# C products of a selective scan in pairs of states, with the sixteen states of a unit dealt anew to VectorE, GpSimd and TensorE

## The chip, the cores and the metric

One core of one Trainium2 chip runs the whole program in one launch. The metric is the time on the device in microseconds, the median of the runs. Engines: TensorE (PE in the profile, PEld its weight loads), VectorE (DVE), ScalarE (ACT), GpSimd (POOL) and SyncE (SP), which issues the transfers.

## The reference, cut to what matters

A layer norm, a scan over channels and a bidirectional selective scan (Mamba) with 2048 inner channels, 16 states, 4096 tokens, then gating and an output projection. The part that the change touches is this, once forward and once backward over the tokens:

```python
def step(h, inp):
    u_t, dt_t, B_t, C_t = inp
    dA = jnp.exp(dt_t[:, :, None] * A)
    h = dA * h + (dt_t * u_t)[:, :, None] * B_t[:, None, :]
    y = jnp.einsum('bdn,bn->bd', h, C_t)
    return (h, y)
```

All data are 32-bit floats.

## The kernel before

The scan stage (`stage_scan`) works in 256 units: 128 of the backward direction, then 128 of the forward one. A unit is one block of 128 channels by one chunk of 512 tokens; 16 units make a chunk. For each state n of 16, ScalarE writes `da` = exp(A·delta) to one of two PSUM slots (L1074), GpSimd has made `w` = du·B for four states in one instruction (L1179), and VectorE runs the scan over the 512 tokens (L1231). Then h times C has to be summed over the states into `yT`, a PSUM tile in which TensorE adds transposes.

Three groups of states do this in three ways:

- VN, ten states: the scan writes `h` in PSUM (two slots), VectorE multiplies by C into one of six `hc` slots (`weigh`, L1241), TensorE adds the transpose (L962).
- PN, four states: the scan writes `hs` in SBUF (four slots shared with TN), GpSimd multiplies by C into `hp` (`weigh_c`, L1188), TensorE adds the transpose (L923).
- TN, two states: the scan writes `hs`, TensorE turns it into `in_ps` (`turn`, L858), ScalarE copies that to `h_turned` (`turn_copy`, L1040), and TensorE multiplies it by a diagonal of C into `yT` (`add_turned`, L867).

Every engine has its own program, in order, with the place of each piece of work given by the state number n at which it stands. On ScalarE, step n of unit b is `save(b, n)` (L1054), which keeps the last column of state n-2 for the next chunk and waits for that scan; then the exponential of state n; then whatever stands at n: at 0 the copy `proj_copy` once a chunk; at 1 the diagonals of the convolution and `dt_read`; at 2 `yT_copy` of the unit before; at 2, 4, 5 and 6 the chain that gives `delta` of the next unit; at 7 `in_copy` (L1014); at 10 `ud` (L1106) and `xc_copy` (L1017); at 12 and 15 the two `turn_copy`. So no exponential is started before all that stands ahead of it, and it is at most two states ahead of the scans.

On TensorE, step n of a unit has: at 0 and 2 the two halves of the input projection (`in_step`, L836), at 5 the convolution (L843), at 8 and 12 the two turns, at 11 the projection `proj` (L848) and `ud` (L954), at 12 and 15 `add_turned` (the one at 12 ahead of the turn at 12), at 13 the `dt` product of a later unit (L831; at 0 in the last unit of a chunk), at the POOL_AT steps the sum of `hp`, and at the end of each step of a VN state the sum of its `hc`, for which the whole queue waits. `in_ps` and `dt_ps` are one PSUM bank each.

GpSimd's unit is: `w` of group 2, C product, `w` of group 3, C product, `u` and `du` of the next unit (L1163, L1166), C product, `w` 0 of the next unit, C product, `w` 1 of the next unit; in the first unit of a chunk two diagonals of C (L1154) besides.

A product of VectorE waits for its scan, for a free `hc` slot, and for the `save` of its state (`h_saved`): the wait names the count of step n+2 of ScalarE, which is the step that saves n.

SyncE issues all loads and stores in program order; it holds for `du_done`, `yT_copied`, `in_copied`, `xc_copied` and `proj_mm` of each unit in that order.

In the last 16 of the backward units (112 to 127) no input projection is left to do; the forward units 128 to 238 have again an input projection (of z) and a convolution for later units.

Of the kernel before, what the change touches and what calls it, by code (L numbers as in the profile page):

```python
# [9 lines left out]
P = 128  # L10
# [7 lines left out]
NS = 16  # L18
# [10 lines left out]
PN = [2, 5, 8, 11]  # L29
TN = [4, 10]  # L30
# [3 lines left out]
NHS = 4  # L34
# [514 lines left out]
def stage_scan(nc, ident, hnT_d, winx_d, winz_d, wx_d, wdt_d, convp_d, par_d, skip_d,  # L549
               x_pad_d, xc_d, z_d, bc_d, yT_d):  # L550
    with Scope(nc, "scan") as sc:
# [18 lines left out]
        delta, u, du = (sc.sb(n, [P, 2, T]) for n in ("delta", "u", "du"))  # L570
# [4 lines left out]
        hs, hp = sc.sb("hs", [P, NHS, T]), sc.sb("hp", [P, NP, T])  # L575
# [43 lines left out]
        def h_slot(b, n):  # L619
            if n in SN:  # L620
                return hs[:, (b * NSN + SN.index(n)) % NHS]
            return h[:, (b * NV + VN.index(n)) % 2]
# [31 lines left out]
        POOL_AT = [5, 8, 11, 14]  # L654
# [171 lines left out]
        def _(pe):  # L826
# [89 lines left out]
            def unit(b):  # L916
                ins = inputs_of(b)
                for n in range(NS):
                    if n in POOL_AT:
                        i = POOL_AT.index(n)  # L920
# [58 lines left out]
        def _(act):  # L979
# [88 lines left out]
            def unit(b):  # L1068
                s, nxt, ins = b % 2, b + 1 < NU, inputs_of(b)
                for n in range(NS):  # L1070
# [11 lines left out]
                    if n == 2:  # L1082
                        yT_copy(b - 1)
# [18 lines left out]
                    if n == 10:  # L1102
                        act.wait_ge(S["skip_loaded"], 2 * DB * LOAD)
                        act.wait_ge(S["u_done"], b + 1)
                        act.wait_ge(S["yT_copied"], b + 1)
                        nc.scalar.activation(ud[:], u[:, s], ACT.Copy,  # L1106
                                             scale=skip[:, block_of(b):block_of(b) + 1]).then_inc(S["ud_done"], 1)
# [39 lines left out]
        def _(pool):  # L1147
# [10 lines left out]
            def scan_input(b):  # L1158

                s = b % 2  # L1160
                pool.wait_ge(p_in[s], (b // 2 + 1) * (NPL * LOAD))
                hold(pool, S["ud_done"], b + 1, S["passed"])
                nc.gpsimd.tensor_scalar(u[:, s], xc[:, s], 10.0, -10.0, ALU.min, ALU.max).then_inc(S["u_done"], 1)  # L1163
                pool.wait_ge(S["u_done"], b + 1)
                pool.wait_ge(S["delta_done"], b + 1)
                nc.gpsimd.tensor_tensor(du[:, s], delta[:, s], u[:, s], ALU.mult).then_inc(S["du_done"], 1)  # L1166

            def weigh_b(b, g, single=False):

                s = b % 2  # L1170
# [3 lines left out]
                if single:  # L1174
                    for i in range(G):
                        nc.gpsimd.tensor_tensor(w[:, g, i], du[:, s], bcast_b[:, g * G + i],
                                                ALU.mult).then_inc(S["w_done"], 1)
                else:
                    nc.gpsimd.tensor_tensor(w[:, g], du[:, s].unsqueeze(1).to_broadcast([P, G, T]),  # L1179
                                            bcast_b[:, g * G:(g + 1) * G], ALU.mult).then_inc(S["w_done"], G)  # L1180

            def weigh_c(b, i):

                n = PN[i]
                pool.wait_ge(c_loaded[n // G], (b // DB + 1) * LOAD)
                pool.wait_ge(S["scan_done"], b * NS + (n + 1 + SCR))
                pool.wait_ge(S["hp_used"], b * NP + i + 1)
                nc.gpsimd.tensor_tensor(hp[:, i], h_slot(b, n), bcast_c[:, n], ALU.mult).then_inc(S["hp_done"], 1)  # L1188

            def unit(b):  # L1190
# [4 lines left out]
                weigh_c(b, 1)  # L1195
                if nxt:
                    scan_input(b + 1)
                weigh_c(b, 2)
# [3 lines left out]
                if nxt:  # L1202
                    weigh_b(b + 1, 0)
                weigh_c(b, 3)
                if nxt:
                    weigh_b(b + 1, 1)

# [10 lines left out]
        def _(dve):  # L1218
            def scan(b, n):
# [14 lines left out]
            def weigh(b, n):  # L1234
                i = VN.index(n)
                dve.wait_ge(c_loaded[n // G], (b // DB + 1) * LOAD)
                dve.wait_ge(S["scan_done"], b * NS + n + 1 + SCR)
                dve.wait_ge(S["hc_used"], b * NV + i + 1)
# [267 lines left out]
```

## Time and profile before

| | |
|---|---|
| median of 3 runs | 8327.16 us (8322.33 to 8331.08) |
| profiled execution, its own time | 8327.64 us |
| its span, first to last instruction | 8325.9 us |
| busy share: TensorE, VectorE, ScalarE, GpSimd | 87%, 87%, 64%, 81% |
| first scan of the stage starts at | 775.6 us |
| last scan starts at | 7279.1 us |
| mean granted TensorE clock | 0.948 |

Busy shares are of the whole span; the scan stage is 78% of it and its own shares are higher. An instruction's duration in the profile is longer than the time until the next one starts, since instructions of one engine overlap by up to 0.1 us; where several follow one another without a wait, the difference of their starts is what one costs. The clock is told as a share of 2.4 GHz; it has two levels, 2.4 and 1.2 GHz, and the figure is the mean over a stretch.

### The profile page before, as it was taken

Reading aid. Unit: us, or ns where it says so; the run is one execution under the profiler, and the core shown is the slowest. Engines: PE = TensorE matmul, PEld = TensorE weight load, DVE = VectorE, ACT = ScalarE, POOL = GpSimd, SP = SyncE. Lnnn points to the kernel's source line nnn. Section 1 sums busy time; section 2 is a strip of 40 time slices with the busy share of each in tenths; the row PEclk is TensorE's granted clock in tenths of the full one; section 3 lists DMA queues with packets and bytes.
Section 4 is the critical chain, followed back from the end, with each engine's and each line's share of the span. In section 5 each row is a group of like instructions: output and inputs, shape, how many; then the busy total and the mean of one; then the engine's idle time right before and its main releaser. Section 6 shows DMA issues by size and latency. Waiting matters only on the chain. (4 is left out here: it accounts for less than half of the span.)

```text
span 8325.9 us, 116063 instructions
## 1 busy us (share of the span) xinstructions
PE 7232.1 (87%) x32656; PEld 4473.8 (54%) x32656; DVE 7202.0 (87%) x7790; ACT 5330.5 (64%) x12487; POOL 6737.9 (81%) x2833
## 2 busy tenths in 40 slices
PE   7568989998999899977899899899888987779999
PEld 3243555555555555555555555555555555534444
DVE  6921999999999999999999999999999999934444
ACT  3743777777777777776777777777777776610000
POOL 0612999999999999999999999999999999921110
PEclk9789999999999999988899999999999998889999
DMA  3273232313232323221323232323232322154342
GB/s 86 76 199 135 66 117 69 117 66 117 69 117 66 117 69 117 67 98 43 105 76 127 80 129 75 128 80 127 76 128 81 124 98 82 44 199 139 134 141 75
DMA packets 540822, 843.96 MB, mean 101 GB/s; under 512 B 112576, under 2 KB 260032, under 8 KB 522816
## 3 DMA queue, kind: packets, MB, share of 16 engines
q1 hardware_dynamic: 540224, 837.03, 30.5%
q8 instruction: 248, 4.06, 0.2%
q14 instruction: 350, 2.87, 0.1%
HBM read 583.83 MB, written 253.02 MB: 101 GB/s over the span
## 5 line engine op out<-in xcount | busy, mean ns | idle before, releaser
L1179 POOL TENSOR_TENSOR scan_w<-scan_du,scan_bcast_b 128x2048 f32<-128x2048 f32 x1023 | 4633.4, 4541 | 3.6 <-DMA scan_bcast_b<-bc 3.6
L1231 DVE TENSOR_TENSOR_SCAN scan_h<-scan_da,scan_state,scan_w 128x512 f32<-128x512 f32 x2560 | 3178.7, 1280 | 36.6 <-ACT scan_da L1074 21.3
L1074 ACT ACTIVATE scan_da<-scan_delta,scan_prm 128x512 f32<-128x512 f32 x4096 | 2804.3, 685 | 0.0
L962 PE MATMUL scan_yT<-all_ident,scan_hc 128*128 128x128 f32 x10240 | 1514.7, 279 | 768.1 <-DVE scan_hc L1241 767.5
L962 PEld LDWEIGHTS scan_yT<-all_ident,scan_hc 128*128 128x128 f32 x10240 | 1184.8, 142 | 1447.9 <-DVE scan_hc L1241 1068.5
L1231 DVE TENSOR_TENSOR_SCAN scan_hs<-scan_da,scan_state,scan_w 128x512 f32<-128x512 f32 x1536 | 1906.1, 1265 | 59.4 <-PE scan_in_ps L858 41.0
L836 PE MATMUL scan_in_ps<-scan_hn,scan_win 128*128 128x512 f32 x3840 | 1730.8, 593 | 13.5 <-issue 13.5
L1241 DVE TENSOR_TENSOR scan_hc<-scan_h,scan_bcast_c 128x512 f32<-128x512 f32 x2560 | 1652.5, 678 | 38.4 <-ACT scan_state L1054 36.7
L1188 POOL TENSOR_TENSOR scan_hp<-scan_hs,scan_bcast_c 128x512 f32<-128x512 f32 x1024 | 1306.5, 1276 | 60.0 <-issue 54.1
L836 PEld LDWEIGHTS scan_in_ps<-scan_hn,scan_win 128*128 128x128 f32 x3840 | 693.1, 191 | 714.7 <-issue 714.7
L1054 ACT ACTIVATE scan_state<-scan_h 128x1 f32<-128x1 f32 x2560 | 433.4, 169 | 868.6 <-DVE scan_h L1231 861.3
L843 PE MATMUL scan_dt_ps<-scan_x,scan_diag 128*128 128x512 f32 x1920 | 899.4, 612 | 1.1 <-ACT scan_x L1014 1.1
L1390 PE MATMUL out_o_ps<-out_yg,out_wout 128*128 128x512 f32 x2048 | 892.6, 595 | 0.0
L1358 POOL TENSOR_TENSOR out_yf<-out_yf,out_yb 128x512 f32<-128x512 f32 x128 | 162.9, 1273 | 740.5 <-DMA out_z<-z 740.5
L923 PE MATMUL scan_yT<-all_ident,scan_hp 128*128 128x128 f32 x4096 | 644.2, 282 | 2.8 <-POOL scan_hp L1188 2.5
L1390 PEld LDWEIGHTS out_o_ps<-out_yg,out_wout 128*128 128x128 f32 x2048 | 386.5, 191 | 465.8 <-issue 465.8
L1368 ACT ACTIVATE out_sz<-out_z 128x512 f32<-128x512 f32 x128 | 80.7, 630 | 822.2 <-DMA out_z<-z 822.2
L867 PE MATMUL scan_yT<-scan_h_turned,scan_c_diag 128*128 128x128 f32 x4096 | 594.4, 293 | 0.0
L843 PEld LDWEIGHTS scan_dt_ps<-scan_x,scan_diag 128*128 128x128 f32 x1920 | 355.9, 196 | 383.9 <-issue 383.9
L867 PEld LDWEIGHTS scan_yT<-scan_h_turned,scan_c_diag 128*128 128x128 f32 x4096 | 560.4, 212 | 0.0
L1040 ACT ACTIVATE scan_h_turned<-scan_in_ps 128x512 f32<-128x512 f32 x512 | 300.6, 587 | 338.4 <-PE scan_in_ps L858 338.4
L923 PEld LDWEIGHTS scan_yT<-all_ident,scan_hp 128*128 128x128 f32 x4096 | 499.2, 146 | 8.2 <-POOL scan_hp L1188 6.8
(128 smaller groups left out, 6761.9 us busy)
## 6 DMA issues: line engine op xcount, KB each, us to landing
yT<-scan_y_out SPq DMA_DIRECT2D x257, 256.0 KB, 2.0
scan_win<-winx SPq DMA_DIRECT2D x128, 512.0 KB, 3.6
xc<-scan_xc_out SPq DMA_DIRECT2D x256, 256.0 KB, 2.0
scan_xc<-xc SPq DMA_DIRECT2D x256, 256.0 KB, 3.9
scan_bcast_b<-bc SPq DMA_DIRECT2D x64, 1024.0 KB, 8.3
scan_bcast_c<-bc SPq DMA_DIRECT2D x64, 1024.0 KB, 7.7
scan_win<-winz SPq DMA_DIRECT2D x128, 512.0 KB, 4.7
scan_x<-x_pad SPq DMA_DIRECT2D x128, 257.5 KB, 2.6
```

The source lines that it names most:

```text
L836: last = nc.tensor.matmul(bank, win[:, s, i], hn[:, i], start=(i == 0), stop=(i == KT - 1))
L843: last = nc.tensor.matmul(bank, diag[:, s, i], x[:, s, at:at + T], start=(i == 0), stop=(i == TAPS - 1))
L867: last = nc.tensor.matmul(yT[:, tb], c_diag[:, k, tb], h_turned[:, tb * P:(tb + 1) * P], start=False, stop=False)
L923: last = nc.tensor.matmul(yT[:, tb], hp[:, i, tb * P:(tb + 1) * P], ident[:], is_transpose=True, start=False, stop=False)
L962: last = nc.tensor.matmul(yT[:, tb], hc_slot(b, n)[:, tb * P:(tb + 1) * P], ident[:], is_transpose=True, start=(i == 0 and tb == 0), stop= ...
L1054: nc.scalar.activation(state_of(unit_, n_), h_slot(unit_, n_)[:, col:col + 1], ACT.Copy).then_inc(S["h_saved"], 1)
L1074: nc.scalar.activation(da[:, n % 2], delta[:, s], ACT.Exp, scale=decay(b, n)).then_inc(S["exp_done"], 1)
L1179: nc.gpsimd.tensor_tensor(w[:, g], du[:, s].unsqueeze(1).to_broadcast([P, G, T]), bcast_b[:, g * G:(g + 1) * G], ALU.mult).then_inc(S["w_d ...
L1188: nc.gpsimd.tensor_tensor(hp[:, i], h_slot(b, n), bcast_c[:, n], ALU.mult).then_inc(S["hp_done"], 1)
L1231: nc.vector.tensor_tensor_scan(flip(b, h_slot(b, n)), flip(b, da[:, n % 2]), flip(b, w[:, n // G, n % G]), state_of(b, n), ALU.mult, ALU.a ...
L1241: nc.vector.tensor_tensor(hc_slot(b, n), h_slot(b, n), bcast_c[:, n], ALU.mult).then_inc(S["hc_done"], 1)
L1390: last = nc.tensor.matmul(o_ps[:, q % 2], wout[:, q, b], yg[:, g, b], start=(b == 0), stop=(b == DB - 1))
```

## The change

- The states are dealt anew: PN = 0, 1, 10, 13; TN = 4, 7; VN = 2, 3, 5, 6, 8, 9, 11, 12, 14, 15, five pairs of neighbours. `hs` has one slot for each of its six states instead of four in turn; `delta` keeps two slots, `u` and `du` have one.
- VectorE multiplies two states by C in one instruction of 128x1024, right after scans 4, 7, 10 and 13, which write SBUF; the pair 14, 15 is multiplied after scan 0 of the next unit. The wait for `h_saved` becomes that for the second state of the pair, n+1.
- GpSimd multiplies 0 and 1 in one instruction and 10 and 13 in another; its order is `w` 2, pair, `w` 3, `u`, `du`, `w` 0, `w` 1, pair.
- TensorE takes `hp` at steps 5, 8, 14, 14 instead of 5, 8, 11, 14.
- ScalarE: `yT_copy` moves from step 2 to 4 and `ud` from 10 to 5. `turn_steps` (the turns at 8 and 12, their copies at 12 and 15) and every other step stay as they are.

```diff
-PN = [2, 5, 8, 11]
-TN = [4, 10]
+PN = [0, 1, 10, 13]
+TN = [4, 7]
...
-NHS = 4
+HS = {0: 0, 1: 1, 4: 2, 7: 3, 10: 4, 13: 5}
...
-        delta, u, du = (sc.sb(n, [P, 2, T]) for n in ("delta", "u", "du"))
+        delta, u, du = sc.sb("delta", [P, 2, T]), sc.sb("u", [P, T]), sc.sb("du", [P, T])
...
-        hs, hp = sc.sb("hs", [P, NHS, T]), sc.sb("hp", [P, NP, T])
+        hs, hp = sc.sb("hs", [P, NSN, T]), sc.sb("hp", [P, NP, T])
...
-                return hs[:, (b * NSN + SN.index(n)) % NHS]
-            return h[:, (b * NV + VN.index(n)) % 2]
+                return hs[:, HS[n]]
+            return h[:, VN.index(n) % 2]
...
-        POOL_AT = [5, 8, 11, 14]
+        POOL_AT = [5, 8, 14, 14]
...
-                    if n == 2:
+                    if n == 4:
                         yT_copy(b - 1)
...
-                    if n == 10:
+                    if n == 5:
                         act.wait_ge(S["skip_loaded"], 2 * DB * LOAD)
...
-                hold(pool, S["ud_done"], b + 1, S["passed"])
-                nc.gpsimd.tensor_scalar(u[:, s], xc[:, s], 10.0, -10.0, ALU.min, ALU.max).then_inc(S["u_done"], 1)
+                hold(pool, S["ud_done"], b + 2, S["passed"])
+                nc.gpsimd.tensor_scalar(u[:], xc[:, s], 10.0, -10.0, ALU.min, ALU.max).then_inc(S["u_done"], 1)
...
             def weigh_c(b, i):
-                n = PN[i]
-                pool.wait_ge(c_loaded[n // G], (b // DB + 1) * LOAD)
-                pool.wait_ge(S["scan_done"], b * NS + (n + 1 + SCR))
-                pool.wait_ge(S["hp_used"], b * NP + i + 1)
-                nc.gpsimd.tensor_tensor(hp[:, i], h_slot(b, n), bcast_c[:, n], ALU.mult).then_inc(S["hp_done"], 1)
+                first, second = PN[i], PN[i + 1]
+                for n in (first, second):
+                    pool.wait_ge(c_loaded[n // G], (b // DB + 1) * LOAD)
+                pool.wait_ge(S["scan_done"], b * NS + (second + 1 + SCR))
+                pool.wait_ge(S["hp_used"], b * NP + i + 2)
+                nc.gpsimd.tensor_tensor(hp[:, i:i + 2], hs[:, HS[first]:HS[first] + 2],
+                                        bcast_c[:, first:second + 1:second - first], ALU.mult
+                                        ).then_inc(S["hp_done"], 2)
             def unit(b):
                 nxt = b + 1 < NU
                 weigh_b(b, 2)
                 weigh_c(b, 0)
                 weigh_b(b, 3)
-                weigh_c(b, 1)
-                if nxt:
-                    scan_input(b + 1)
-                weigh_c(b, 2)
                 if b % DB == 0:
                     for k in range(NTN):
                         make_diagonal(b, k)
                 if nxt:
+                    scan_input(b + 1)
                     weigh_b(b + 1, 0)
-                weigh_c(b, 3)
-                if nxt:
                     weigh_b(b + 1, 1)
+                weigh_c(b, 2)
...
-                if n in SN:
-                    g = b * NSN + SN.index(n) - NHS
-                    if g >= 0 and SN[g % NSN] in PN:
-                        dve.wait_ge(S["hp_done"], g // NSN * NP + PN.index(SN[g % NSN]) + 1 + NP)
-                    elif g >= 0:
-                        dve.wait_ge(S["h_turn_mm"], g // NSN * NTN + TN.index(SN[g % NSN]) + 1)
-                else:
+                if n in PN:
+                    dve.wait_ge(S["hp_done"], b * NP + PN.index(n) + 1)
+                elif n in TN and b:
+                    dve.wait_ge(S["h_turn_mm"], (b - 1) * NTN + TN.index(n) + 1)
+                elif n in VN:
                     dve.wait_ge(S["hc_done"], b * NV + VN.index(n) + 1)
...
+            def weigh(b, i):
+
+                n, at = VN[i], (b * NV + i) % NOUT
+                for m in (n, n + 1):
+                    dve.wait_ge(c_loaded[m // G], (b // DB + 1) * LOAD)
+                dve.wait_ge(S["scan_done"], b * NS + n + 2 + SCR)
+                dve.wait_ge(S["hc_used"], b * NV + i + 2)
                 if b + 1 < NU or n < NS - 2:
-                    dve.wait_ge(S["h_saved"], b * NS + n + 3)
+                    dve.wait_ge(S["h_saved"], b * NS + n + 4)
+                nc.vector.tensor_tensor(hc[:, at:at + 2], h[:], bcast_c[:, n:n + 2], ALU.mult).then_inc(S["hc_done"], 2)
             def unit(b):
                 for n in range(NS):
                     scan(b, n)
-                    if n in PN:
-                        ready = (n - 2, n - 1)
-                    else:
-                        ready = (n - 1, n) if n in (NS - 3, NS - 1) else ()
-                    for m in ready:
-                        if m in VN:
-                            weigh(b, m)
+                    if n == 0 and b:
+                        weigh(b - 1, NV - 2)
+                    if n in (4, 7, 10, 13):
+                        weigh(b, (n - 4) // 3 * 2)
```

## Rows read from the trace of the kernel before

**Rows 1.** Busy time by window: units 16 to 111, 112 to 127, 128 on

```profile
1180.00:3620.00 2440.00, 2200.14 (x10804) 1412.51 (x10803) 2413.43 (x2516) 1870.64 (x4553) 2414.72 (x982) 0.97 0.28 95
3624.00:4061.00 437.00, 315.64 (x1543) 220.58 (x1541) 401.75 (x418) 299.54 (x740) 400.43 (x163) 0.81 0.19 63
4061.00:7256.00 3195.00, 2828.84 (x14070) 1849.32 (x14069) 3165.66 (x3303) 2425.26 (x5895) 3166.21 (x1287) 0.96 0.29 98
```

**Rows 2.** The same windows, scans of L1231 alone (x is their count)

```profile
1180.00:3620.00 2440.00, 1887.90 (x1548) 0.97 0.28 95
3624.00:4061.00 437.00, 312.55 (x257) 0.81 0.19 63
4061.00:7256.00 3195.00, 2477.56 (x2033) 0.96 0.29 98
```

**Rows 3.** Groups by line and form: 512-wide and 1024-wide products, whole span

```profile
L1241 DVE TENSOR_TENSOR scan_hc<-scan_h,scan_bcast_c 128x512 f32<-128x512 f32 x2560 | 1652.5, 678 | 38.4 <-ACT scan_state L1054 36.7 <-issue 0.3
...
L347 DVE TENSOR_TENSOR norm_xn<-n_scanned,n_xt 128x1024 f32 (+1 forms) x32 | 37.2, 1203 | 0.0
...
L302 POOL TENSOR_TENSOR norm_xn<-norm_xn,norm_rstd 128x1024 f32 x28 | 65.4, 2355 | 0.0
```

**Rows 4.** Longest wait of VectorE in the scan stage: us in total, times, longest

```profile
DVE scan_hs L1231 <- PE scan_in_ps L858: 41.0, 66, 1.9
```

**Rows 5.** Timeline of VectorE, end of unit 50

```profile
2078.87 2.46 DVE L1231 TENSOR_TENSOR_SCAN scan_h<-scan_da,scan_state,scan_w 128x512 f32<-128x512 f32 x2
2081.23 1.27 DVE L1241 TENSOR_TENSOR scan_hc<-scan_h,scan_bcast_c 128x512 f32<-128x512 f32 x2
2082.42 2.46 DVE L1231 TENSOR_TENSOR_SCAN scan_h<-scan_da,scan_state,scan_w 128x512 f32<-128x512 f32 x2
...
2085.97 1.28 DVE L1231 TENSOR_TENSOR_SCAN scan_h<-scan_da,scan_state,scan_w 128x512 f32<-128x512 f32 x1
```

**Rows 6.** Timeline of GpSimd, unit 50

```profile
2067.73 4.53 POOL L1179 TENSOR_TENSOR scan_w<-scan_du,scan_bcast_b 128x2048 f32<-128x2048 f32 x1
2072.22 1.26 POOL L1188 TENSOR_TENSOR scan_hp<-scan_hs,scan_bcast_c 128x512 f32<-128x512 f32 x1
...
2075.49 1.28 POOL L1188 TENSOR_TENSOR scan_hp<-scan_hs,scan_bcast_c 128x512 f32<-128x512 f32 x1
```

**Rows 7.** Timeline of TensorE, unit 50

```profile
2062.81 3.60 PE L836 MATMUL scan_in_ps<-scan_hn,scan_win 128*128 128x512 f32 x8
2066.25 1.04 PE L962 MATMUL scan_yT<-all_ident,scan_hc 128*128 128x128 f32 x8
...
2071.56 3.67 PE L843 MATMUL scan_dt_ps<-scan_x,scan_diag 128*128 128x512 f32 x8
...
2079.01 0.66 PE L962 MATMUL scan_yT<-all_ident,scan_hc 128*128 128x128 f32 x4 [2.03 <-DVE scan_hc L1241]
2079.50 0.60 PE L923 MATMUL scan_yT<-all_ident,scan_hp 128*128 128x128 f32 x4
...
2081.23 1.06 PE L867 MATMUL scan_yT<-scan_h_turned,scan_c_diag 128*128 128x128 f32 x8
2082.12 0.60 PE L858 MATMUL scan_in_ps<-all_ident,scan_hs 128*128 128x128 f32 x4
...
2083.09 1.12 PE L831 MATMUL scan_dt_ps<-scan_proj,scan_wdt 64*128 64x512 f32 x2
```

**Rows 8.** Timeline of ScalarE, unit 50: copies, saves and exponentials

```profile
2070.82 0.60 ACT L1014 ACTIVATE scan_x<-scan_in_ps 128x512 f32<-128x512 f32 x1 [0.60 <-PE scan_in_ps L836]
2071.31 0.17 ACT L1054 ACTIVATE scan_state<-scan_h 128x1 f32<-128x1 f32 x1
2071.36 0.70 ACT L1074 ACTIVATE scan_da<-scan_delta,scan_prm 128x512 f32<-128x512 f32 x1
...
2082.76 0.60 ACT L1040 ACTIVATE scan_h_turned<-scan_in_ps 128x512 f32<-128x512 f32 x1 [0.65 <-PE scan_in_ps L858]
```

**Rows 9.** Timeline of TensorE in unit 122, where the clock is lower

```profile
3907.50 5.30 PE L843 MATMUL scan_dt_ps<-scan_x,scan_diag 128*128 128x512 f32 x8
```

More of the change, by code:

```diff
@@ L918, in unit @@
                 for n in range(NS):
-                    if n in POOL_AT:
-                        i = POOL_AT.index(n)
+                    for i in range(NP):
+                        if n != POOL_AT[i]:
+                            continue
                         pe.wait_ge(S["hp_done"], b * NP + i + 1 + NP)
@@ L1105, in unit @@
                         act.wait_ge(S["yT_copied"], b + 1)
-                        nc.scalar.activation(ud[:], u[:, s], ACT.Copy,
+                        nc.scalar.activation(ud[:], u[:], ACT.Copy,
                                              scale=skip[:, block_of(b):block_of(b) + 1]).then_inc(S["ud_done"], 1)
@@ L1161, in scan_input @@
                 pool.wait_ge(p_in[s], (b // 2 + 1) * (NPL * LOAD))
-                hold(pool, S["ud_done"], b + 1, S["passed"])
-                nc.gpsimd.tensor_scalar(u[:, s], xc[:, s], 10.0, -10.0, ALU.min, ALU.max).then_inc(S["u_done"], 1)
+                hold(pool, S["ud_done"], b + 2, S["passed"])
+                nc.gpsimd.tensor_scalar(u[:], xc[:, s], 10.0, -10.0, ALU.min, ALU.max).then_inc(S["u_done"], 1)
                 pool.wait_ge(S["u_done"], b + 1)
                 pool.wait_ge(S["delta_done"], b + 1)
-                nc.gpsimd.tensor_tensor(du[:, s], delta[:, s], u[:, s], ALU.mult).then_inc(S["du_done"], 1)
+                nc.gpsimd.tensor_tensor(du[:], delta[:, s], u[:], ALU.mult).then_inc(S["du_done"], 1)
             def weigh_b(b, g, single=False):
-                s = b % 2
                 pool.wait_ge(S["du_done"], b + 1)
@@ L1175, in weigh_b @@
                     for i in range(G):
-                        nc.gpsimd.tensor_tensor(w[:, g, i], du[:, s], bcast_b[:, g * G + i],
+                        nc.gpsimd.tensor_tensor(w[:, g, i], du[:], bcast_b[:, g * G + i],
                                                 ALU.mult).then_inc(S["w_done"], 1)
                 else:
-                    nc.gpsimd.tensor_tensor(w[:, g], du[:, s].unsqueeze(1).to_broadcast([P, G, T]),
+                    nc.gpsimd.tensor_tensor(w[:, g], du[:].unsqueeze(1).to_broadcast([P, G, T]),
                                             bcast_b[:, g * G:(g + 1) * G], ALU.mult).then_inc(S["w_done"], G)
             def weigh_c(b, i):
-                n = PN[i]
-                pool.wait_ge(c_loaded[n // G], (b // DB + 1) * LOAD)
-                pool.wait_ge(S["scan_done"], b * NS + (n + 1 + SCR))
-                pool.wait_ge(S["hp_used"], b * NP + i + 1)
-                nc.gpsimd.tensor_tensor(hp[:, i], h_slot(b, n), bcast_c[:, n], ALU.mult).then_inc(S["hp_done"], 1)
+                first, second = PN[i], PN[i + 1]
[6 more added lines that the diff above has]
+                                        ).then_inc(S["hp_done"], 2)
             def unit(b):
@@ L1232, in scan @@
                                              state_of(b, n), ALU.mult, ALU.add).then_inc(S["scan_done"], 1)
[L1234 to L1238, printed above, removed]
+            def weigh(b, i):
[4 more added lines that the diff above has]
+                dve.wait_ge(S["hc_used"], b * NV + i + 2)
                 if b + 1 < NU or n < NS - 2:
-                    dve.wait_ge(S["h_saved"], b * NS + n + 3)
-                nc.vector.tensor_tensor(hc_slot(b, n), h_slot(b, n), bcast_c[:, n], ALU.mult).then_inc(S["hc_done"], 1)
+                    dve.wait_ge(S["h_saved"], b * NS + n + 4)
+                nc.vector.tensor_tensor(hc[:, at:at + 2], h[:], bcast_c[:, n:n + 2], ALU.mult).then_inc(S["hc_done"], 2)
             def unit(b):
@@ L1266, in _ @@
                 unit(b)
+            weigh(NU - 1, NV - 2)
 def stage_out(nc, passed, ident, yf_d, yb_d, z_d, wout_d, x1T_d, out_d):
```

## The prediction

> **What bounds the kernel now.** I read the page first. Over the span no engine stands out: TensorE and VectorE are busy alike and GpSimd is close (the table of busy shares). The windows of the scan stage alone say more. In the ordinary stretches VectorE is busy 2413 of 2440 us and 3166 of 3195, and GpSimd is busy 2415 and 3166 [rows 1]. Two engines are full together, TensorE has 10% to spare, ScalarE a quarter. With the counts of scans (1548 and 2033, 16 to a unit) a unit takes 5635 / 223.8 = 25.18 us there, and 437 / 16.06 = 27.2 in the stretch without an input projection, where TensorE's granted clock is 0.81 [rows 2]. The waits of VectorE are few: 41 us for the turn that frees an `hs` slot (1.9 us a time, in the stretch with the lower clock above all) and 37 us ahead of the products for a `save` of ScalarE [rows 3, 4].
>
> The work of a unit is summed from starts, so that overlaps count. VectorE: two scans cost 2081.23 - 2078.87 = 2.36, two products 1.19 [rows 5]. So 16 x 1.18 + 10 x 0.595 = 24.8 us. GpSimd: a `w` of four states costs 4.49, a C product 1.23 (its 1.27 less the 0.04 of overlap that `w` shows), and one product with `u` and `du` 3.27 [rows 6]. So 4 x 4.49 + 3.27 + 3 x 1.23 = 24.92, and with the two diagonals once in 16 units 25.07. GpSimd is the nearer bound of 25.18; VectorE is 0.4 under it.
>
> **The products themselves.** On VectorE a product of 1024 lasts 1.203 us, one of 512 0.678 [rows 3]. The pair costs 0.595 + 0.525 = 1.12 instead of 1.19; five save 0.35 and a unit of VectorE falls to 18.88 + 5.6 = 24.45. On GpSimd 1024 elements last 2.355 [rows 3], 2.31 after overlap; two pairs save 4 x 1.23 - 2 x 2.31 = 0.30, so 24.62, with the diagonals 24.77.
>
> Here the page "VectorE: DVE Perf Modes" of the Trainium skill (section on the TRN2 errata) bears on the case: a fixed latency is paid once per instruction, and an fp32 tensor_tensor takes (N+151) cycles at 0.96 GHz. By that each instruction saved would give 0.157 us and five 0.79; by the rows a pair gives 0.07, since neighbours overlap. I use the rows.
>
> **The other edits that cost or give little.** Six `hs` slots remove the wait of 41 us. GpSimd's new order has room: the pair 10, 13 waits for scan 13 and holds back `w` 2 of the next unit, which is wanted only by scan 8; the pair 0, 1 waits for scan 1 and holds `w` 3, wanted by scan 12. From scan 13's end GpSimd needs 2.3 + 4.5 and then waits for scan 1 with nothing lost at periods over 24.8. Single `u` and `du` hold `scan_input` for `ud`, now five steps earlier: free. On SyncE `load_p` waits for `du` as before; the stores of y come 2 us later, behind `yT_copied`, with `store_x` and `store_xc` queued behind; a unit has 25 us for them, so nothing. `yT_copy` at step 4 waits for the sums of 14, 15, which are ready about a microsecond before (below): without the move it would stall.
>
> **Where the new order costs: the end of a unit.** I count from the end of the product of 11 and 12, which follows scan 13. TensorE's queue stands at step 11, at the sum of `hc` 11. Only behind it come, at step 12, `add_turned` of state 4 and then the turn of state 7. ScalarE's copy of that turn stands at step 15, ahead of the exponential of state 0 of the next unit, and scan 0 needs that. So: the sum starts 0.05 later and costs 0.49 (2079.50 - 2079.01), `add_turned` 0.89 (2082.12 - 2081.23), the turn ends 0.60 after its start [rows 7]; the copy starts 0.04 later (2082.76 after 2082.72), 0.49 to the `save`, 0.05 to the exponential, 0.70 for it [rows 8], 0.04 until the scan. Sum 3.35. VectorE itself has in this time only scans 14 and 15, 2.36 less 0.09 (the product's end lies that far behind the next start): 2.27. **Stall 1.07 us a unit.** Before, the turn came after the sum of state 9, and the products of 14 and 15 stood between scan 15 and the next unit: the same copy started at 2082.76, 3.2 us ahead of scan 0 at 2085.97 [rows 5, 8], where 1.3 is needed. The cover was those products and the earlier turn, and both are gone.
>
> **The middle of a unit.** Count from scan 0. The product of 14 and 15 starts at 1.18 and ends at 2.38. TensorE's sums of 14 and 15 with `add_turned` between: 2.43 + 0.49 + 0.89 + 0.44 = 4.25. Only then comes the next input projection, 2 x 3.44 (2066.25 - 2062.81), its end at 11.28. Before, both products were over when scan 0 began, so the projection started some 2.4 earlier. VectorE meanwhile: scan 1 at 2.30, scans 2, 3, 4, product, scans 5, 6, 7, product of 5 and 6 due at 11.68. That product needs the `save` of 6, at step 8 of ScalarE, behind `in_copy` at step 7: 11.28 + 0.04 + 0.49 + 0.17 [rows 8] + 0.04 = 12.02. **Stall 0.34.** Then TensorE sums 2 and 3 (0.87) and `hp` (0.44) and runs the convolution (3.67): from 11.13 to 16.11. `xc_copy` stands at step 10, the `save` of 9 behind it: 16.11 + 0.04 + 0.6 + 0.17 + 0.04 = 16.96; the product of 8 and 9 is due at 12.02 + 1.12 + 3.54 = 16.68. **Stall 0.28.** Where the clock is full no other exponential is late: two steps of ScalarE with one extra activation each take 1.3 a step, and a scan with its share of a product 1.5.
>
> **Sum.** 24.45 + 1.07 + 0.34 + 0.28 = 26.14 us. Once in 16 units the `dt` product (1.05, 2083.09 in [rows 7] and its 1.12) goes ahead of the input projection and shifts both middle stalls: 0.07 on the mean, 26.21. Against 25.18 that is +1.03 x 240 ordinary units = +247 us. The 16 units of the lower clock have no input projection, so the middle stalls are absent; their turn wait goes; the end chain costs 1.07, or 0.87 more if TensorE's 1.98 of it run at 5.30 / 3.67 [rows 7, 9]. About 25.9 for 27.2: -21.
>
> One term the rows of a full clock leave out: TensorE's clock. It is busy 5029 of 5635 us now, 22.5 a unit, 0.89, with a clock of 0.965; in the other stretch 0.72 with 0.81 [rows 1]. At 26.2 a unit the share is 0.86; on the line between the two the clock is 0.93, so some 6% more of the time is at 1.2 GHz. A unit wholly there would take 10.5 x 0.44 for projection and convolution and 0.87 for the end chain, 5.5 us more: 0.34 a unit, 82 us. Part of it falls where TensorE waits anyway; the bounds are 0 and 82, I take 40. All told 8328 + 247 - 21 + 40 = 8594, say 8590 (the profiled execution's own time of 8327.6 is the median within half a microsecond). Own range: each stall is known to about 0.15 (60 us together), the clock term 0 to 82: 8520 to 8680.
>
> **Rivals.**
> (A) Faster. The waits do not bind and the sums of the two full engines decide: VectorE 24.45, GpSimd 24.77. Then 240 x 0.41 + 16 x 2.4 = 137 us less, 8190. It needs the exponential of state 0 at most 2.27 us after the product of 11 and 12, that is a turn of state 7 that TensorE runs before the sum of 11. The queue in the code does not allow it; for it speaks that GpSimd, the fullest engine, is relieved. 0.09, with all that I may misread.
> (B) The end chain alone binds, the projection and convolution are in time (they lack 0.3 each): 24.45 + 1.07 = 25.52, +0.34 x 240 - 21 = +61, 8390. 0.14.
> (C) The clock falls more than on the line. The new idle time of TensorE is in two pieces, some 2.4 us ahead of the sum of 11 and 1.4 ahead of that of 14, against one of 2.03 [rows 7]; the first lies just ahead of the end chain. At a clock of 0.90, 13% more of the time at 1.2 GHz: 0.72 x 240 = +172 on 8554, 8725; at 0.81, 8960. 0.12.
> The page "TensorE: Matmul & The Clock Gate" of the Trainium skill (Part 1) says that the slow state is the default and that activity releases it; the 0.81 beside TensorE's lower busy share agrees [rows 1].
>
> **How the numbers follow.** Forecast 0.65, A 0.09, B 0.14, C 0.12. The range from 8385 to 8730 leaves out A and the slow half of C. A measurement of this kernel can tell 0.2% (17 us) from no change; no case lies there, but the lower side of B reaches it if the end chain is half as long: I give 0.04 of B's chance to the same and 0.01 to faster. Faster 0.10, same 0.04, slower 0.86.
>
> **What the profile after will show.** Products x1280 of 1.2 us on VectorE and x512 of 2.36 on GpSimd. VectorE's waits: scans of state 0 (an `hs` scan now) for ScalarE's `da`, about 1 us a unit and 250 in total; products waiting for ScalarE's `save`, twice 0.3 a unit. No wait for the turn. ScalarE's wait for the turn (L1040) and TensorE's for `hc` grow. VectorE and GpSimd both fall to some 94% of the stage. A scan 0 that starts 2.4 us after the product of 11 and 12 ends would make the prediction wrong; so would an input projection that starts before 3 us.

## The result, and the profile after

8899.75 us median of 4 runs (8897.35 to 8902.79) against 8325.49, the median of now 4 runs of the kernel before: 1.0689 times the time before, 95% interval 1.0671 to 1.0708. I had forecast 8590, with a range of 8385 to 8730. The sign and the two places in an ordinary unit were right; the 264 us that I had added were less than half of the 574 that came.

The windows of the profile after, over units 16 to 111, 112 to 127 and 128 to 239 for all engines, and then those and the units from 240 on with the scans of L1228 alone (the x of VectorE, 16 to a unit):

```profile
1240.00:3876.00 2636.00, 2211.50 (x10727) 1443.62 (x10726) 2402.58 (x2015) 1818.66 (x4510) 2374.09 (x780) 0.96 0.25 84
3877.00:4313.00 436.00, 290.21 (x1536) 209.98 (x1535) 398.96 (x336) 296.34 (x736) 395.16 (x130) 0.90 0.19 64
4314.00:7397.00 3083.00, 2586.39 (x12534) 1687.80 (x12534) 2805.26 (x2352) 2123.81 (x5265) 2772.92 (x911) 0.96 0.28 94
```

```profile
1240.00:3876.00 2636.00, 1864.83 (x1535) 0.96 0.25 84
3877.00:4313.00 436.00, 310.99 (x256) 0.90 0.19 64
4314.00:7397.00 3083.00, 2177.66 (x1792) 0.96 0.28 94
7397.00:7850.00 453.00, 310.41 (x256) 0.86 0.15 51
```

VectorE and GpSimd, full before [rows 1], are busy 91% and 90%. A unit takes 2636 / 95.9 = 27.5 us and 3083 / 112 = 27.5 where it took 25.2 [rows 2], 436 / 16 = 27.3 in the middle stretch where it took 27.2, and 453 / 16 = 28.3 in the last one. The mean granted clock of the ordinary stretches is as before, 0.96.

The groups by line, and the waits of VectorE in the scan stage:

```profile
L1240 DVE TENSOR_TENSOR scan_hc<-scan_h,scan_bcast_c 128x1024 f32<-128x1024 f32 x1280 | 1539.1, 1202 | 105.2 <-PE scan_yT L963 57.8 <-ACT scan_state L1055 46.4 <-DVE scan_h L1228 0.2
...
L1189 POOL TENSOR_TENSOR scan_hp<-scan_hs,scan_bcast_c 128x1024 f32<-128x1024 f32 x512 | 1206.5, 2356 | 585.5 <-DVE scan_hs L1228 583.9 <-issue 0.2
```

```profile
DVE scan_hs L1228 <- ACT scan_da L1075: 420.5, 257, 3.3
DVE scan_hc L1240 <- PE scan_yT L963: 57.8, 215, 1.3
DVE scan_hc L1240 <- ACT scan_state L1055: 46.4, 28, 2.7
```

The products last what the 1024-wide rows of other stages said, 1.202 and 2.356 [rows 3]. The wait for the turn [rows 4] is gone. In its place scans into `hs` wait 257 times for the exponential, once a unit, 420 us in all: that is scan 0. Of the waits ahead of products, 57.8 us are laid to the sum of an `hc` slot and 46.4 to a save; below I show that the save is the true one for both.

VectorE through unit 50 (start, duration, instruction), to set beside [rows 5]:

```profile
2175.12 1.28 DVE L1228 TENSOR_TENSOR_SCAN scan_hs<-scan_da,scan_state,scan_w 128x512 f32<-128x512 f32 x1 [2.20 <-ACT scan_da L1075]
2176.32 1.20 DVE L1240 TENSOR_TENSOR scan_hc<-scan_h,scan_bcast_c 128x1024 f32<-128x1024 f32 x1
2177.43 1.27 DVE L1228 TENSOR_TENSOR_SCAN scan_hs<-scan_da,scan_state,scan_w 128x512 f32<-128x512 f32 x1
...
2182.15 1.20 DVE L1240 TENSOR_TENSOR scan_hc<-scan_h,scan_bcast_c 128x1024 f32<-128x1024 f32 x1
2183.45 2.46 DVE L1228 TENSOR_TENSOR_SCAN scan_h<-scan_da,scan_state,scan_w 128x512 f32<-128x512 f32 x2
...
2187.31 1.22 DVE L1240 TENSOR_TENSOR scan_hc<-scan_h,scan_bcast_c 128x1024 f32<-128x1024 f32 x1 [0.23 <-PE scan_yT L963]
...
2192.22 1.20 DVE L1240 TENSOR_TENSOR scan_hc<-scan_h,scan_bcast_c 128x1024 f32<-128x1024 f32 x1
...
2197.07 1.20 DVE L1240 TENSOR_TENSOR scan_hc<-scan_h,scan_bcast_c 128x1024 f32<-128x1024 f32 x1
2198.37 2.47 DVE L1228 TENSOR_TENSOR_SCAN scan_h<-scan_da,scan_state,scan_w 128x512 f32<-128x512 f32 x2
2201.62 1.28 DVE L1228 TENSOR_TENSOR_SCAN scan_hs<-scan_da,scan_state,scan_w 128x512 f32<-128x512 f32 x1 [0.78 <-ACT scan_da L1075]
```

This unit takes 26.50 us (2201.62 - 2175.12). The next takes 28.02, and so on in turn: by the starts of the first scans, 209 ordinary units have a mean of 27.28 (25.10 before), and of them 101 take more than 27.5. Two things are to be seen here. The product that starts at 2176.32 is followed 1.11 us later by a scan into `hs`; the one at 2182.15 is followed 1.30 later by a scan into `h`, and so are those at 2192.22 and 2197.07 (after the one at 2187.31, which itself waited, it is 1.36). And from the end of the product of 11 and 12 (2197.07 + 1.20) to scan 0 it is 3.35 us.

TensorE and ScalarE at the end of unit 50 (first four rows) and of unit 51 (the rest):

```profile
2198.32 0.66 PE L963 MATMUL scan_yT<-all_ident,scan_hc 128*128 128x128 f32 x4 [2.47 <-DVE scan_hc L1240]
2198.82 1.06 PE L867 MATMUL scan_yT<-scan_h_turned,scan_c_diag 128*128 128x128 f32 x8
2199.71 0.60 PE L858 MATMUL scan_in_ps<-all_ident,scan_hs 128*128 128x128 f32 x4
...
2200.35 0.60 ACT L1041 ACTIVATE scan_h_turned<-scan_in_ps 128x512 f32<-128x512 f32 x1 [2.38 <-PE scan_in_ps L858]
...
2224.83 1.11 PE L963 MATMUL scan_yT<-all_ident,scan_hc 128*128 128x128 f32 x4 [2.46 <-DVE scan_hc L1240]
2225.74 1.91 PE L867 MATMUL scan_yT<-scan_h_turned,scan_c_diag 128*128 128x128 f32 x8
2227.44 0.88 PE L858 MATMUL scan_in_ps<-all_ident,scan_hs 128*128 128x128 f32 x4
...
2228.36 0.60 ACT L1041 ACTIVATE scan_h_turned<-scan_in_ps 128x512 f32<-128x512 f32 x1 [3.89 <-PE scan_in_ps L858]
```

The chain is the same, but in unit 51 TensorE's part lasts 3.49 us instead of 1.99. Four microseconds of each by windows (the figure behind the last engine is the granted clock):

```profile
2224.00:2228.00 4.00, 3.17 (x15) 3.17 (x16) 3.24 (x3) 0.48 (x1) 4.00 (x2) 0.57 0.47 166
2198.00:2202.00 4.00, 3.67 (x24) 2.75 (x25) 3.11 (x4) 1.65 (x5) 4.00 (x2) 1.00 0.33 92
```

In unit 51 the clock is 0.57 over the chain, that is 1.2 GHz for nearly all of it, right after 2.46 us without work. Ahead of the chain of unit 50 there is the same idle time, and it ran at 2.4 GHz. The trace's granted clock says the same of all units: the 101 long ones of the 209 each have a stretch at 1.2 GHz (28.08 us on the mean), the 108 others have none (26.53 us). In the kernel before 74 of the 209 have such a stretch too, but they take only 25.38 us against 24.95 for the rest.

### The profile page after: what moved, and what is told of

It is laid out like the page before. It is cut to its first block and busy times, and to the rows that moved or that the text cites. A ratio compares the mean times of both kernels' runs of the same rounds, so it can differ in the third digit from the quotient of the medians.

```text
span 8895.6 us, 112992 instructions
## 1 busy us (share of the span) xinstructions
PE 7317.9 (82%) x32656; PEld 4578.2 (51%) x32656; DVE 7226.4 (81%) x6510; ACT 5249.4 (59%) x12487; POOL 6688.5 (75%) x2321
## 3 DMA queue, kind: packets, MB, share of 16 engines
q1 hardware_dynamic: 540224, 837.03, 28.3%
## 5 line engine op out<-in xcount | busy, mean ns | idle before, releaser
L1228 DVE TENSOR_TENSOR_SCAN scan_h<-scan_da,scan_state,scan_w 128x512 f32<-128x512 f32 x2560 | 3150.5, 1276 | 135.5 <-ACT scan_da L1075 16.0
L963 PE MATMUL scan_yT<-all_ident,scan_hc 128*128 128x128 f32 x10240 | 1543.9, 288 | 1257.5 <-DVE scan_hc L1240 1257.5
L1228 DVE TENSOR_TENSOR_SCAN scan_hs<-scan_da,scan_state,scan_w 128x512 f32<-128x512 f32 x1536 | 1941.7, 1264 | 439.8 <-ACT scan_da L1075 420.5
L963 PEld LDWEIGHTS scan_yT<-all_ident,scan_hc 128*128 128x128 f32 x10240 | 1215.8, 147 | 1703.1 <-DVE scan_hc L1240 1453.4
L836 PE MATMUL scan_in_ps<-scan_hn,scan_win 128*128 128x512 f32 x3840 | 1692.3, 593 | 14.4 <-issue 13.5
L1189 POOL TENSOR_TENSOR scan_hp<-scan_hs,scan_bcast_c 128x1024 f32<-128x1024 f32 x512 | 1206.5, 2356 | 585.5 <-DVE scan_hs L1228 583.9
L1240 DVE TENSOR_TENSOR scan_hc<-scan_h,scan_bcast_c 128x1024 f32<-128x1024 f32 x1280 | 1539.1, 1202 | 105.2 <-PE scan_yT L963 57.8
L867 PE MATMUL scan_yT<-scan_h_turned,scan_c_diag 128*128 128x128 f32 x4096 | 674.1, 319 | 0.0
L867 PEld LDWEIGHTS scan_yT<-scan_h_turned,scan_c_diag 128*128 128x128 f32 x4096 | 629.9, 234 | 0.0
L924 PE MATMUL scan_yT<-all_ident,scan_hp 128*128 128x128 f32 x4096 | 595.1, 279 | 0.2
L924 PEld LDWEIGHTS scan_yT<-all_ident,scan_hp 128*128 128x128 f32 x4096 | 467.6, 143 | 185.2 <-issue 175.6
```

What stands on the lines that cost most here:

```text
L836: last = nc.tensor.matmul(bank, win[:, s, i], hn[:, i], start=(i == 0), stop=(i == KT - 1))
L867: last = nc.tensor.matmul(yT[:, tb], c_diag[:, k, tb], h_turned[:, tb * P:(tb + 1) * P], start=False, stop=False)
L963: last = nc.tensor.matmul(yT[:, tb], hc_slot(b, n)[:, tb * P:(tb + 1) * P], ident[:], is_transpose=True, start=(i == 0 and tb == 0), stop= ...
L1189: nc.gpsimd.tensor_tensor(hp[:, i:i + 2], hs[:, HS[first]:HS[first] + 2], bcast_c[:, first:second + 1:second - first], ALU.mult).then_inc( ...
L1228: nc.vector.tensor_tensor_scan(flip(b, h_slot(b, n)), flip(b, da[:, n % 2]), flip(b, w[:, n // G, n % G]), state_of(b, n), ALU.mult, ALU.a ...
L1240: nc.vector.tensor_tensor(hc[:, at:at + 2], h[:], bcast_c[:, n:n + 2], ALU.mult).then_inc(S["hc_done"], 2)
```

## Experiments

Two theories. **The end chain**: the sum of `hc` 11, `add_turned`, turn, ScalarE's copy and the exponential of state 0, with a clock term on top. **The rival**: the loss is in the middle of the unit and in the pairs themselves. Each run is a time and a ratio to runs of the kernel before made beside it.

### e1: the turn of state 7 one step earlier

```diff
-            return dict(mm=(8, 12), copy=(12, NS - 1), add=(12, NS - 1))
+            return dict(mm=(8, 11), copy=(12, NS - 1), add=(12, NS - 1))
```

> Theory (the end chain): the turn of state 7 stands behind the sum of hc 11 on TensorE, and scan 0 of the next unit waits for its copy. With the turn one step earlier, ahead of that sum, the 420 us that hs scans wait for the exponential go to under 30 and a unit takes 25.6 to 25.9 us: 8400 (8350 to 8480). Rival (the loss is the product's write that the next scan into the same PSUM slot waits for, 0.19 us four times a unit, and the middle of the unit): the wait moves to another place and the time stays above 8700.

Measured 8810.8 us, 1.0581 (1.0550 to 1.0612): far outside my range, and above 8700 as the rival had it. The wait of scan 0 went from 420 to 252 us, not to 30. TensorE and ScalarE at the end of unit 133:

```profile
4435.17 1.53 PE L867 MATMUL scan_yT<-scan_h_turned,scan_c_diag 128*128 128x128 f32 x8
...
4436.80 0.60 ACT L1041 ACTIVATE scan_h_turned<-scan_in_ps 128x512 f32<-128x512 f32 x1 [2.47 <-PE scan_yT L867]
```

The copy now waits for L867, `add_turned` of state 4. There is one `h_turned`, and `turn_copy` waits until it is used (`h_turned_used`); that product still stood behind the sum of `hc` 11. The chain has two links, and I had seen one. The clock hides part of what the first gives: it was 0.917 over this run against 0.945 for the changed kernel, 195 of the 209 ordinary units have a stretch at 1.2 GHz, and the 14 without one take 26.23 us, where the changed kernel takes 26.53.

### e7: both links moved

```diff
-            return dict(mm=(8, 12), copy=(12, NS - 1), add=(12, NS - 1))
+            return dict(mm=(8, 11), copy=(12, NS - 1), add=(11, NS - 1))
```

> On TensorE both the product of state 4 (add_turned) and the turn of state 7 stand at step 11, ahead of the sum of hc 11; the change has both at 12. The run with the turn alone at 11 left ScalarE's copy waiting for add_turned, which frees h_turned. Theory (the end chain): scan 0 waits for nothing of TensorE's; 25.6 us for a unit at full clock, up to 26.3 where the clock falls and delays the input projection; 8450 (8380 to 8540). Rival (the loss sits in the middle of the unit and in the pairs): above 8700.

Measured 8574.3 us, 1.0299 (1.0237 to 1.0361), 325 us under the changed kernel, but above my range. The end of unit 57 and scan 0 of 58:

```profile
2318.76 1.20 DVE L1240 TENSOR_TENSOR scan_hc<-scan_h,scan_bcast_c 128x1024 f32<-128x1024 f32 x1
2320.05 2.47 DVE L1228 TENSOR_TENSOR_SCAN scan_h<-scan_da,scan_state,scan_w 128x512 f32<-128x512 f32 x2
2322.43 1.26 DVE L1228 TENSOR_TENSOR_SCAN scan_hs<-scan_da,scan_state,scan_w 128x512 f32<-128x512 f32 x1
```

Scan 0 (2322.43) follows the two scans of 14 and 15 without a gap. Most units take 25.6 us, as expected. What I priced too low are units at 27.25 (a stretch at 1.2 GHz begins some 2 to 3 us after their scan 0, the input projection is late, the product of 5 and 6 waits 1.6 us; 46 of the 209 have such a stretch) and the last units of a chunk, 29.0 on the mean of 13; before they took 26.2.

### e2 and e6: work for TensorE in the idle time ahead of the chain

```diff
+                        for _ in range(5):          # e2; range(2) in e6
+                            nc.tensor.matmul(yT[:].rearrange("p a b -> p (a b)"), zeros[:, 0:P], zeros[:],
+                                             start=False, stop=False)
```

The products add zeros to `yT`, behind `ud` at step 11.

> Five 512-wide products with a zero weight tile are added into yT after ud, in TensorE's idle time of 2.5 us ahead of the sum of hc 11 (they add zeros). Theory (every second unit is 1.5 us longer because that idle time drops TensorE to 1.2 GHz just where the end chain runs): all units become 26.5 us, the slow ones at chunk borders shorter too, 8620 (8570 to 8680), granted clock higher. Rival (the alternation comes from slots or semaphores that repeat every two units): units keep alternating 26.5 and 28.1, 8900 or more.

Measured 9082.0 us, 1.0907 (1.0875 to 1.0939). The alternation was gone, all ordinary units take 28.1 us; but I had taken one such product for 0.43 us, and five last 4.3, not 2.15: the chain starts behind them. So the same with two.

> As the run with five products of zeros, with two: they take 1.7 us of TensorE's 2.47 us of idle time ahead of the sum of hc 11, where five took 4.3 and were themselves waited for. Theory (that idle time puts TensorE at 1.2 GHz for the end chain in every second unit, at 1.5 us a time): ordinary units all take 26.5 us, 8680 (8620 to 8740). Rival (the alternation has another cause): 26.5 and 28.1 still alternate, 8900.

Measured 8666.1 us, 1.0409 (1.0379 to 1.0439). TensorE before the chain of a unit:

```profile
2151.58 1.88 PE L959 MATMUL scan_yT<-scan_zeros 128*128 128x512 f32 x4
2154.21 0.66 PE L967 MATMUL scan_yT<-all_ident,scan_hc 128*128 128x128 f32 x4 [0.75 <-DVE scan_hc L1245]
2154.71 1.06 PE L868 MATMUL scan_yT<-scan_h_turned,scan_c_diag 128*128 128x128 f32 x8
```

The same window of the run and of the changed kernel, with the granted clock behind the last engine:

```profile
1180.00:3900.00 2720.00, 2420.08 (x11740) 1508.41 (x11739) 2555.21 (x2144) 1933.43 (x4796) 2528.81 (x831) 0.99 0.26 89
1180.00:3900.00 2720.00, 2276.39 (x11036) 1485.90 (x11036) 2477.23 (x2078) 1878.02 (x4658) 2448.94 (x805) 0.96 0.26 88
```

Ordinary units take 26.5 us, all of them, against 26.5 and 28.0 in turn, and none has a stretch at 1.2 GHz. With this work TensorE is idle for 0.75 instead of 2.46 us ahead of the chain, nothing else in the loop is changed, and that gives back 234 us (8900 - 8666). The clock term is shown.

### e8: one product of zeros on top of e7

> The run before with one product of zeros (0.86 us) into yT ahead of the sum of hc 11. Theory (what the end chain leaves over is the clock): fewer units above 25.7 us, 20 to 80 us less than without it. Rival (with the chain out of the way the clock no longer matters): the same time within 15 us.

Measured 8566.9 us, 1.0290 (1.0218 to 1.0363): no difference that the runs can tell from e7. Some units of 27.25 remain, elsewhere. Inconclusive.

### e3: the copy of the input projection behind the save

```diff
-        NORMAL = dict(into=(0, 2), diag=1, copy=7, conv=5, xc=10, proj=11)
+        NORMAL = dict(into=(0, 2), diag=1, copy=8, conv=5, xc=10, proj=11)
```

> ScalarE's copy of the input projection stands at step 8 instead of 7, behind the save of state 6. Theory (the late input projection holds the product of 5 and 6 by 0.31 us a unit through that save): the gap ahead of this product goes, of it 0 to 0.15 comes back at the product of 8 and 9: minus 40 to minus 75 us, 8825 to 8860. Rival (the gap is the write of an hc slot or the scan itself): no change.

Measured 8872.0 us, 1.0655 (1.0624 to 1.0686), an interval that overlaps that of the change. The timeline decides:

```profile
2187.44 1.20 DVE L1240 TENSOR_TENSOR scan_hc<-scan_h,scan_bcast_c 128x1024 f32<-128x1024 f32 x1
...
2192.59 1.22 DVE L1240 TENSOR_TENSOR scan_hc<-scan_h,scan_bcast_c 128x1024 f32<-128x1024 f32 x1 [0.19 <-PE scan_yT L963]
```

ScalarE's copy from the convolution and the save of 9 in the same run:

```profile
2191.71 0.69 ACT L1018 ACTIVATE scan_xc_out<-scan_dt_ps,scan_convp 128x512 f32<-128x512 f32 x1 [0.86 <-PE scan_dt_ps L843]
2192.30 0.16 ACT L1055 ACTIVATE scan_state<-scan_h 128x1 f32<-128x1 f32 x1
```

The product of 5 and 6 has lost its gap, so the save behind the copy was what it waited for, whatever releaser the profile names; and the product of 8 and 9 now waits instead, for the save behind `xc_copy`: it starts 0.13 us after that save ends (2192.46). The two middle stalls I had counted stand one behind the other: with one gone the other appears.

### e4: singles in the changed order

```diff
-                nc.vector.tensor_tensor(hc[:, at:at + 2], h[:], bcast_c[:, n:n + 2], ALU.mult).then_inc(S["hc_done"], 2)
+                for j in range(2):
+                    nc.vector.tensor_tensor(hc[:, at + j], h[:, j], bcast_c[:, n + j], ALU.mult).then_inc(S["hc_done"], 1)
```

TensorE waits for both products of a pair (`(i | 1) + 3`).

> VectorE's pairs are two products of 512 again, in the same order of states; TensorE waits for both of a pair as after the change, so the end chain keeps its start. Theory (a pair's write is waited for by the scan that follows into the same slots, so a pair costs 1.30 us where two singles cost 1.19): 4 x -0.11 + 0.075 = -0.37 a unit, minus 95 us, 8805 (8770 to 8840). Rival (pairs save instructions and the 0.10 gaps are harmless or belong to the order of states): plus 0.35 a unit, 8990.

Measured 8887.5 us, 1.0673 (1.0642 to 1.0704): no gain that the intervals show. Two singles that do not wait cost 1.18 where a pair costs 1.30, but the product of 5 and 6 then waits longer (0.35 instead of 0.23) for the same save:

```profile
2194.03 1.29 DVE L1241 TENSOR_TENSOR scan_hc<-scan_h,scan_bcast_c 128x512 f32<-128x512 f32 x2 [0.35 <-ACT scan_state L1055]
2195.24 2.46 DVE L1228 TENSOR_TENSOR_SCAN scan_h<-scan_da,scan_state,scan_w 128x512 f32<-128x512 f32 x2
```

From scan 0 to the product of 8 and 9 it is 17.10 us in both kernels: TensorE's input projection and convolution, not VectorE, set this stretch. My expectation added a saving off that path. The totals of e3 and e4 also carry the clock: a unit without a stretch at 1.2 GHz takes 26.48 and 26.47 us against 26.53, but 118 and 116 units are over 27.5 us instead of 101. Neither total measures its edit alone.

### e9: VectorE's pairs alone, in the kernel before

```diff
+HV = {0: 0, 1: 1, 3: 0, 6: 0, 7: 1, 9: 0, 12: 0, 13: 1, 14: 0, 15: 1}
...
+                    for m, k in {2: [(0, 2)], 5: [(3, 1)], 8: [(6, 2)], 11: [(9, 1)], 13: [(12, 2)], 15: [(14, 2)]}.get(n, []):
+                        weigh(b, m, k)
```

> The kernel before with one part of the change alone: VectorE's products of states 0 and 1, 6 and 7, 12 and 13, 14 and 15 in pairs, 3 and 9 single, right after scans 2, 5, 8, 11, 13, 15 (five hc slots, so that a pair never wraps). Theory (a pair costs 1.30 and not 1.12 where a scan into its PSUM slots follows, and the pairs after 13 and 15 wait for their own scan and the save besides): 0.3 to 0.9 us a unit longer, 8400 to 8560. Rival (fewer instructions are less time): 8250 to 8300.

Measured 8768.2 us, 1.0532 (1.0501 to 1.0562), 443 us over the kernel before, nearly twice the most that I expected (8560): 26.68 us for most ordinary units. VectorE through the end of unit 51:

```profile
2194.42 0.67 DVE L1251 TENSOR_TENSOR scan_hc<-scan_h,scan_bcast_c 128x512 f32<-128x512 f32 x1
2195.22 2.47 DVE L1235 TENSOR_TENSOR_SCAN scan_h<-scan_da,scan_state,scan_w 128x512 f32<-128x512 f32 x2
2198.02 1.23 DVE L1248 TENSOR_TENSOR scan_hc<-scan_h,scan_bcast_c 128x1024 f32<-128x1024 f32 x1 [0.34 <-ACT scan_state L1056]
2199.35 2.47 DVE L1235 TENSOR_TENSOR_SCAN scan_h<-scan_da,scan_state,scan_w 128x512 f32<-128x512 f32 x2
```

A product whose slot the next scan takes costs 0.80 alone and 1.33 as a pair, where unhindered ones cost 0.59 and 1.11; and a pair right behind its own scan starts 0.34 late, for the save of its second state. My slot map puts states 3 and 9 in the slot of the pair that follows, so the singles pay too. Pairing on VectorE with two PSUM slots costs time in this order of states, and the change's order, which has no such singles, avoids the 0.34 but not the 1.30 of four pairs.

### e5 and e10: what of the change pays

e5 is the kernel before with six fixed `hs` slots, single `u` and `du`, `ud` at step 5, `hp` taken at steps 8, 8, 14, 14, and GpSimd's pairs (2, 5) and (8, 11) in this order:

```diff
             def unit(b):
+                weigh_c(b, 0)
+                scan_input(b + 1)
+                weigh_b(b + 1, 0)
+                weigh_c(b, 2)
+                for g in range(1, NG):
+                    weigh_b(b + 1, g)
```

> The kernel before (its states, VectorE's single products) with one part of the change alone: six fixed hs slots, single u and du, ud at step 5, and GpSimd's products in pairs (2, 5) and (8, 11), its order being pair, u, du, w 0, pair, w 1, w 2, w 3 so that no pair waits long. Theory (GpSimd's 25.07 us a unit is the nearer bound of the kernel before, and the pairs save it 0.30): 24.8 to 24.95 a unit, the units 112 to 127 lose their wait for the turn: 8215 (8190 to 8270). Rival (VectorE and the copies on ScalarE bound it, GpSimd follows): only the wait for the turn goes, 8270 to 8310.

Measured 8268.7 us, **0.9936 (0.9919 to 0.9952)**: 0.6% faster than the kernel before, at the slow edge of what I expected. e10 is the same with GpSimd's single products and its order as before.

> The kernel before with six fixed hs slots, single u and du and ud at step 5, GpSimd's order and its single products as before: the run with pairs on GpSimd less the pairs. Theory (half of that run's gain is the relief of GpSimd, half the wait for the turn that goes): the units 112 to 127 fall from 27.2 us as there, the ordinary units stay at 25.1: 8295 (8280 to 8310). Rival (the slots give it all): 8270, as with the pairs.

Measured 8291.7 us, 0.9954 (0.9938 to 0.9971). By the starts of the first scans, units 112 to 127 take 27.3 before, 26.2 in e10, 25.7 in e5; ordinary units 25.10, 25.02, 24.96. So the slots (with the single `u` and `du` and the earlier `ud`) give most of it. Whether GpSimd's pairs and their order add something stays open: the two intervals overlap.

## Why the prediction was off, point by point

- **The products' own durations** were right: 1.202 and 2.356. **Their cost on VectorE was not.** I took 1.12 from start to start (and added 18.88 + 5.6 to 24.45, where it is 24.48: 7 us in all). It is 1.11 only where a scan into `hs` follows; where a scan into `h` follows it is 1.30, since that scan waits for the product that has just been issued to free its slot, and the overlap of neighbours is lost. I listed the waits that the change adds, but not this one, because it is between instructions of one engine. It does not cost that four times. Unit 50 takes 26.50 us where my sum was 26.14: 0.18 of it is the pair of 8 and 9 itself, 0.14 lies before that pair, where TensorE's work sets the pace, as e4 shows, and behind the pair of 11 and 12 the end chain is the longer one anyway.
- **The end of a unit**: 3.35 us from the product of 11 and 12 to scan 0, as predicted to the hundredth at the full clock. I named `add_turned` as work ahead of the turn; that the copy waits for it a second time, through the one `h_turned`, I missed. It changes nothing in the forecast, but e1 and rival A were built on it.
- **The middle**: the input projection predicted at 4.25 after scan 0, measured 4.27 (2179.39, shown below, less 2175.12); the product of 5 and 6 predicted at 12.02 after scan 0, measured 12.19; that of 8 and 9 at 16.96, measured 17.10. The second stall does not show as a gap, since the slower pairs bring the product there at the same time.
- **TensorE's clock**, the step that failed. I put 40 us for it, by two steps, and neither held. The first was a mean clock of 0.93 from a line between the busy shares and the mean clocks of two stretches. The mean clock stayed where it was, 0.96; but what time at 1.2 GHz there is falls on the chain that everything waits for, in every second ordinary unit, 1.5 us each: (27.28 - 26.50) x 209 = 163 us. The second was the price of work at 1.2 GHz, 5.30 / 3.67 [rows 9]. Those 5.30 us were only in part at 1.2 GHz, as the granted clock over them says, 0.68:

```profile
3907.50:3912.80 5.30, 5.30 (x11) 2.23 (x11) 5.27 (x6) 2.35 (x6) 5.13 (x4) 0.68 0.00 0
```

So I had 0.87 us more for the slow chain, where it was 1.50 (3.49 - 1.99). I had even named the idle time (rival C: 2.4 us just ahead of the chain; measured 2.46), yet priced it by a mean. The whole of the term is what e6 gives back, 234 us: by the starts of the units 0.75 x 209 = 157 in the ordinary ones, 2.2 x 13 = 29 in the last units of chunks, 1.0 x 16 = 16 in units 112 to 127 and 2.05 x 16 = 33 in units 239 to 254. The page "TensorE: Matmul & The Clock Gate" of the Trainium skill (Part 1) says that activity is what releases the clock; e6, where work in that gap brought the full clock, agrees. Why it is every second unit and not every one is not settled.
- **The edges**: the last units of 13 chunks went from 26.2 to 30.9 us, 60 us where I had 17. In the unit ahead of them there is no `dt` product at step 13, so TensorE idles 2.45 us ahead of the sum of 14 as well. TensorE in unit 47 (scan 0 at 2088.79) and, last row, in unit 50 (scan 0 at 2175.12):

```profile
2091.24 0.93 PE L963 MATMUL scan_yT<-all_ident,scan_hc 128*128 128x128 f32 x4 [2.45 <-DVE scan_hc L1240]
...
2095.82 7.13 PE L836 MATMUL scan_in_ps<-scan_hn,scan_win 128*128 128x512 f32 x16
...
2179.39 7.03 PE L836 MATMUL scan_in_ps<-scan_hn,scan_win 128*128 128x512 f32 x16
```

Right behind that idle time the clock is low (0.93 us for a sum that takes 0.66 at 2.4 GHz). The sums of 14 and 15 with `add_turned` take 3.43 us instead of 1.82, the `dt` product comes behind them, and the input projection starts 7.03 us after scan 0, not 4.27; it runs at the full clock itself. The product of 5 and 6 waits 2.7 us. Units 112 to 127 stayed at 27.3 (I had 25.9, 21 us less in all): the wait for the turn went, but scan 0 now waits 1.8 us on the mean for the end chain. Units 239 to 254 went from 25.5 to 28.7 where I had nothing beyond the ordinary loss (about 35 us).

Sum of the measured terms against before: (27.28 - 25.10) x 209 = 456, 4.6 x 13 = 60, 0, 3.2 x 16 = 51, together 567 of 574 us: the ordinary units, the last units of 13 chunks, units 112 to 127 (nothing) and units 239 to 254. In place of the forecast's 264 the misses add 80 for the ordinary unit at the full clock (0.33 x 240, 26.54 against 26.21), 163 less 40 for the clock in the ordinary units, and some 100 at the edges. Of these 100 the larger part is the clock again, by the e6 figures above. The fit is closer than the bookkeeping deserves: the kernel before already had 0.43 x 74 = 32 us in its units with a stretch at 1.2 GHz.

**Rivals.** A was off. It named the place of the turn as its condition, which was right but not all: with the turn alone ahead (e1) scan 0 still waits 252 us, with both links moved (e7) it waits 7 us in all, though the unit is then at 25.6 and not at 24.8, for the middle and the pairs remain. B is excluded: the input projection and the middle lie where they were put. C had the place right and its level wrong: its 8725 and 8960 hung on mean clocks of 0.90 and 0.81 that never came in the ordinary stretches, and it is luck that the 8900 measured lies between them. The view of the kernel before that GpSimd's 25.07 us was its nearer bound was too strong: with its work cut by 0.30 (e5 against e10) an ordinary unit loses 0.06.

## What to carry to other kernels

Before an operation moves away from the end of a loop body, ask what its time was covering: here two products hid a chain through two other engines, and they went while the chain also started later. Look for every link by which a step waits, buffers included, and price a moved chain at both clocks if an idle time stands ahead of it: mean clocks say little about the place where the slow time falls. Joining two instructions saved time here (0.07 us a pair) only where nobody waited for the result at once; with as many slots as the pair fills, the next writer does wait.

## What the runs showed that I had not expected

- An instruction of VectorE that waits for the one just before it on the same engine starts 0.10 to 0.14 us after its end, where an independent one starts 0.08 to 0.09 before it: 1.30 against 1.11 us from start to start for 1024 elements, 0.80 against 0.59 for 512.
- Two 512-wide products of zeros in an idle gap of TensorE made the whole kernel 234 us faster than the changed one without them (8666 against 8900). What a stretch at 1.2 GHz costs depends on what runs in it: the ordinary units that had one were 0.43 us longer in the kernel before and 1.55 us longer in the changed one.
- The profile lays the wait of the product of 5 and 6 to the sum of its `hc` slot, which was free since long; moving the copy behind the save (e3) showed that it was the save.
